# AdaLN block with causal attention: bias product in two halves, another order in the first and last unit, VectorE makes batch 1's unrounded rows from the banks, and another split of the last product

## What is computed

```python
mod = (silu(c) @ wmod).reshape(2, 6, 1, 256)          # sa, ca, ga, sb, cb, gb
ga, gb = ((2 * (g >= 0) - 1) * maximum(abs(g), 0.25) for g in (ga, gb))
h = layernorm(x) * (1 + ca) + sa
q, k = rotary((h @ Wq + bq) * 128 ** -0.5), rotary(h @ Wk + bk)
attn = softmax(causal(q @ k.T)) @ (h @ Wv + bv)        # 16 heads
x = x + ga * (attn @ Wo + bo)
h = layernorm(x) * (1 + cb) + sb
x = x + gb * qlinear(silu(qlinear(h, gate)) * qlinear(h, up), down)   # 704 hidden, integer weights less 128
```

## Time and profile before

| | |
|---|---|
| median of three runs | 1036.28 us |
| the profiled execution | 1035.97 us |
| its span | 1034.2 us |
| TensorE busy | 1006.3 us, 97% |
| VectorE, ScalarE, GpSimd busy | 771.6, 678.5, 620.3 us |
| granted clock of TensorE, mean | 0.997 |

### The profile page before, as it was taken

One profiled execution on the slowest core, in us unless ns is written; L12 is line 12 of the kernel. 1 busy time (PEld: TensorE's weight loads), 2 busy tenths in 40 slices (PEclk: granted clock), 3 DMA queues, 4 the chain that ended last, 5 costly groups with the idle time before them and its releaser, 6 DMA issues.

```text
span 1034.2 us, 20453 instructions
## 1 busy us (share of the span) xinstructions
PE 1006.3 (97%) x6318; PEld 903.9 (87%) x6318; DVE 771.6 (75%) x1664; ACT 678.5 (66%) x1447; POOL 620.3 (60%) x472
## 2 busy tenths in 40 slices
...
GB/s 253 120 41 70 44 32 42 72 44 38 37 35 71 51 41 32 67 44 41 41 43 60 41 41 42 71 51 31 32 70 51 41 37 91 62 62 42 1 42 43
DMA packets 41987, 56.03 MB, mean 54 GB/s; under 512 B 5508, under 2 KB 25028, under 8 KB 41924
## 3 DMA queue, kind: packets, MB, share of 16 engines
...
## 4 chain that ended last, share of the span: by engine, by line
PE 91%; DVE 2%; issue 2%; ACT 2%; POOL 1%; DMA 1%; SPq 0%; DVEq 0%; ACTq 0%; POOLq 0%
PE ps_r L1362 18%; PE ps_r L1361 18%; PE ps_r L1360 17%; PE ps_t L1519 12%; PE ps_s L1362 7%; PE ps_s L1361 7%; PE ps_s L1360 6%; PE ps_s L1367 2%; PE ps_s L1370 1%; PE ps_r L1369 1%; PE ps_r L1367 1%; PE ps_r L1458 1%; DMA wmod_a<-in_L_wmod 1%; POOL y L695 0%; ACT probs L907 0%
## 5 line engine op out<-in xcount | busy, mean ns | idle before, releaser
L651 POOL TENSOR_TENSOR swapped<-swapped,sin_sb 128x512 f32<-128x512 f32 x124 | 166.1, 1340 | 236.1 <-DMA swapped<-straight 235.6
L896 ACT ACTIVATE pT_hi<-ps_t 128x512 fp32r<-128x512 f32 (+3 forms) x384 | 186.8, 491 | 85.2 <-PE ps_t L1519 83.1
L1198 DVE TENSOR_TENSOR pT_lo<-ps_t,pT_hi 128x512 fp32r<-128x512 f32 (+3 forms) x384 | 202.3, 550 | 53.7 <-ACT pT_hi L896 53.6
L1263 DVE CUSTOM_DVE_ANT_0 ps_s<-ps_s,mask_wide 128x128 f32<-128x128 f32 (+7 forms) x256 | 194.5, 760 | 55.8 <-PE ps_s L1362 41.6
L661 POOL TENSOR_TENSOR qk_lo<-straight,qk_hi 128x512 fp32r<-128x512 f32 x124 | 162.2, 1322 | 112.3 <-ACT qk_hi L802 112.3
L907 ACT ACTIVATE probs<-ps_s,neg_max 128x128 f32<-128x128 f32 (+7 forms) x256 | 190.3, 743 | 44.1 <-DVE neg_max L1263 37.0
L1519 PE MATMUL ps_t<-ident,probs 128*128 128x128 f32 x1152 | 185.6, 274 | 6.5 <-DVE pT_lo L1198 5.9
L652 POOL TENSOR_TENSOR straight<-straight,cos_sb 128x512 f32<-128x512 f32 x124 | 180.9, 1459 | 0.0
L1126 DVE TENSOR_TENSOR straight<-straight,swapped 128x512 f32<-128x512 f32 x126 | 129.1, 1025 | 32.5 <-POOL straight L652 32.0
L1519 PEld LDWEIGHTS ps_t<-ident,probs 128*128 128x128 f32 x1152 | 134.3, 140 | 11.3 <-issue 4.9
L1360 PE MATMUL ps_s<-qk_hi 128*128 128x512 f32 (+3 forms) x384 | 139.9, 364 | 0.1
...
## 6 DMA issues: line engine op xcount, KB each, us to landing
...
```

The source lines that it names most:

```text
L651: pool.tensor_tensor(swapped[:, q, :], swapped[:, q, :], sin_sb[:, cs], ALU.mult)
L896: nc.scalar.activation(turned_at(ORDER[step], k0, k1)(pT_hi), ps_t[:, (T_FIRST[step] + j) % 2, 0:(k1 - k0) * P].rearrange("p (k q) -> p k ...
L1198: nc.vector.tensor_tensor(turned_at(t, k0, k1)(pT_lo), ps_t[:, (T_FIRST[step] + j) % 2, 0:(k1 - k0) * P].rearrange("p (k q) -> p k q", q=P ...
L1263: nc.vector.tensor_tensor_reduce(rows, rows, mask_wide[:, SEQ - n_keys:SEQ], -1.0, -MASKED, ALU.add, ALU.min, accum_out=neg_max[:, t:t + 1 ...
```

## The change

In unit 0 the bias product is made in two pieces, B0 ahead of the first turn and B1 behind the second; VectorE adds `bo` to the first and the first to the second; ScalarE's and VectorE's lists are reordered; the fourth exponential no longer waits for a turn. For batch 1, ScalarE writes only `hT_hi`; VectorE writes `h32` from the bank with one tensor_scalar (`h_plain`) ahead of each remainder, and TensorE waits for it (`plain_ready`) before it uses the bank again. In unit 31, W10 and W11 are made behind D1 and D2, W11 of unit 30 is summed in `ENDING`, and sums stand behind maxima and turns. In the feed-forward part the third chunk's turns stand one step later and its remainders ahead of steps 9 and 10. GpSimd converts the third part of the down weights earlier and leaves the last remainder to VectorE. The last down product goes by tiles 0 to 2 over the first four parts, then by tiles over the rest.

```diff
@@ -56,8 +56,8 @@
 EARLY_NORMAL_AT = {9: 3}
-TURN_AT = {7: (4,), 8: (5,), 13: (6,), 14: (7,)}
-LOW_AT = {0: (2,), 1: (3,), 8: (4, 5), 14: (6,), 15: (7,)}
+TURN_AT = {8: (4,), 9: (5,), 13: (6,), 14: (7,)}
+LOW_AT = {0: (2,), 1: (3,), 9: (4,), 10: (5,), 14: (6,), 15: (7,)}
@@ -96,13 +96,12 @@
     TENSOR_PLAN: """make:P0- make:P1- mods:1 scores:0 xn:4 make:K0+ xn:5 scores:1 make:Q0+ xn:6 xn:7 scores:2 scores:3
-        make:B turn:0.0 turn:1.0 scores:4 turn:1.1 make:K1+ turn:2.0 scores:5 make:Q1+ turn:3.0 turn:3.1 make:V0
+        make:B0 turn:0.0 turn:1.0 make:B1 scores:4 turn:1.1 make:K1+ turn:2.0 scores:5 make:Q1+ turn:3.0 turn:3.1 make:V0
         turn:4.0 scores:6 make:V1 turn:5.0 scores:7 turn:5.1""",
-    SCALAR_PLAN: """exp:0 out:K0+ xout:4 xout:5 exp:1 out:Q0+ xout:6 xout:7 exp:2 exp:3 high:K0+ high:Q0+ turn:0.0
-        turn:1.0 exp:4 turn:1.1 out:K1+ turn:2.0 exp:5 out:Q1+ turn:3.0
-        turn:3.1 turn:4.0 high:V0 high:K1+ high:V1 turn:5.0 exp:6 split:O turn:5.1 high:Q1+""",
-    VECTOR_PLAN: """max:0 max:1 xlow:4 xlow:5 max:2 max:3 add:K0+ xlow:6 xlow:7 add:Q0+ sum:B turn:0.0
-        turn:1.0 max:4 turn:1.1 gates:0 turn:2.0 max:5 turn:3.0 add:K1+ turn:3.1
+    SCALAR_PLAN: """exp:0 out:K0+ xout:4 xout:5 exp:1 out:Q0+ xout:6 xout:7 exp:2 turn:0.0 exp:3 turn:1.0 high:K0+ high:Q0+
+        turn:1.1 exp:4 out:K1+ turn:2.0 turn:3.0 exp:5 turn:3.1 out:Q1+ turn:4.0 high:V0 high:K1+ high:V1 turn:5.0 exp:6 split:O turn:5.1 high:Q1+""",
+    VECTOR_PLAN: """max:0 max:1 xlow:4 xlow:5 max:2 max:3 add:K0+ xlow:6 xlow:7 turn:0.0 sum:B0 turn:1.0 add:Q0+ sum:B1
+        turn:1.1 max:4 gates:0 turn:2.0 max:5 turn:3.0 add:K1+ turn:3.1
@@ -123,13 +122,13 @@
         make:P1- scores:3 turn:1.0 make:W00- make:X scores:4 turn:1.1 turn:2.0 make:W01- scores:5 make:D0 turn:3.0
-        make:W10- turn:3.1 turn:4.0 make:W11- scores:6 make:D1 turn:5.0 scores:7 make:D2 turn:5.1""",
+        make:D1 turn:3.1 scores:6 make:D2 turn:4.0 make:W10- scores:7 turn:5.0 make:W11- turn:5.1""",
     SCALAR_PLAN: """out:K0+ exp:7- turn:6.0- exp:0 out:Q0+ turn:7.0- turn:7.1- high:P0- turn:0.0 exp:1 exp:2
-        high:P1- turn:1.0 turn:1.1 exp:3 turn:2.0 exp:4 gated:0 out:D0 turn:3.0
-        exp:5 turn:3.1 turn:4.0 out:D1 exp:6 turn:5.0 out:D2 turn:5.1""",
+        high:P1- turn:1.0 turn:1.1 exp:3 turn:2.0 exp:4 gated:0 turn:3.0 out:D0
+        exp:5 turn:3.1 out:D1 turn:4.0 out:D2 exp:6 turn:5.0 turn:5.1""",
     VECTOR_PLAN: """largest:3 max:0 turn:6.0- turn:7.0- turn:7.1- max:1 low:P0- max:2 turn:0.0 moments:0
-        low:P1- max:3 sum:W00- turn:1.0 width:X max:4 turn:1.1 turn:2.0 sum:W01- max:5 turn:3.0 sum:W10- turn:3.1 turn:4.0
-        sum:W11- max:6 max:7 turn:5.0 turn:5.1"""}
+        low:P1- max:3 turn:1.0 sum:W00- width:X max:4 turn:1.1 turn:2.0 max:5 sum:W01- turn:3.0 turn:3.1
+        max:6 turn:4.0 max:7 turn:5.0 sum:W10- turn:5.1"""}
@@ -138,7 +137,7 @@
         silu:4 gu:3 silu:5 gu:4""",
-    VECTOR_PLAN: """turn:6.0- turn:7.0- turn:7.1- moments:1 newton:0 low:P0- low:P1- sum:W00- sum:W01-
+    VECTOR_PLAN: """turn:6.0- turn:7.0- turn:7.1- sum:W11-- moments:1 newton:0 low:P0- low:P1- sum:W00- sum:W01-
@@ -158,7 +157,7 @@
         what, name = token.rstrip("+-").split(":")
-        v = u + {"+": 1, "-": -1}.get(token[-1], 0)
+        v = u + token.count("+") - token.count("-")
@@ -679,7 +679,7 @@
-                        pool.wait_ge(attn_bias_ready, 1)
+                        pool.wait_ge(attn_bias_ready, 2)
@@ -742,9 +742,9 @@
             down_high(1)
+            down_high(2)
...
             gate_rows(2)
-            down_high(2)
@@ -760,6 +760,8 @@
                 low = gu_lo[:, n % GU, :]
+                if n == NCH * HM - 1:
+                    break
@@ -846,7 +848,8 @@
                 src, shift, gain = ps_t[:, n % 2, :], mod[:, k, b:b + 1], mod[:, KT + k, b:b + 1]
-                nc.scalar.activation(h32[:, n % 4, :], src, ACT.Identity, bias=shift, scale=gain)
+                if n < GROUPS4 // 2:
+                    nc.scalar.activation(h32[:, n % 4, :], src, ACT.Identity, bias=shift, scale=gain)
@@ -901,7 +904,7 @@
                 act.wait_ge(max_ready, ps.tiles(u, step + 1))
-                if u * NQ + step >= 3:
+                if u * NQ + step > 3:
@@ -1101,7 +1104,18 @@
             nc.vector.tensor_scalar(bq_s[:, :], cols[:, COL_BQ:COL_BQ + HEADS], SCALE, None, ALU.mult).then_inc(bq_ready, 1)
+            def h_plain(n):
+
+                k, b = n % KT, n // KT // 2
+                dve.wait_ge(hhi_ready, n + 1)
+                dve.wait_ge(hT_ready, n - 3)
+                nc.vector.tensor_scalar(h32[:, n % 4, :], ps_t[:, n % 2, :], mod[:, KT + k, b:b + 1], mod[:, k, b:b + 1],
+                                        ALU.mult, ALU.add).then_inc(plain_ready, 1)
+
             def h_low(n):
+                if n >= GROUPS4 // 2:
+                    h_plain(n)
+                    dve.wait_ge(plain_ready, n - GROUPS4 // 2 + 1)
@@ -1175,7 +1189,11 @@
                 dve.wait_ge(wo_all_ready, 32)
-                nc.vector.tensor_tensor(y[:, 0, :], ps_r[:, ps.bank(piece), 0:DIM], bo_wide[:, :], ALU.add)\
+                more = bo_wide[:, :]
+                if piece[1] == 1:
+                    dve.wait_ge(attn_bias_ready, 1)
+                    more = y[:, 0, :]
+                nc.vector.tensor_tensor(y[:, 0, :], ps_r[:, ps.bank(piece), 0:DIM], more, ALU.add)\
@@ -1194,6 +1212,9 @@
                 k0, k1 = groups_of(t)[j]
+                if u * T_UNIT + T_FIRST[step] + j == T_FIRST[1]:
+
+                    dve.wait_ge(hT_ready, GROUPS4)
@@ -1347,6 +1368,11 @@
                     finish(2 * j, 2, ps_r[:, j % 2, :].rearrange("p (t n) -> p t n", t=2))
+            last = NCH * HM - 1
+            dve.wait_ge(gu_hi_ready, last + 1)
+            dve.wait_ge(gu_split, last)
+            nc.vector.tensor_tensor(gu_hi[HLAST:P, last % GU, :], gu_at(last, HLAST),
+                                    gu_hi[0:HLAST, last % GU, :].bitcast(F32), ALU.subtract).then_inc(gu_split, 1)
@@ -1454,9 +1480,10 @@
                     pe.wait_ge(wo_all_ready, 32)
-                    for h in range(HEADS):
+                    half = HEADS // 2
+                    for h in range(piece[1] * half, piece[1] * half + half):
                         ins = nc.tensor.matmul(dst[:, 0:DIM], cols[:, COL_BV + h:COL_BV + h + 1].broadcast_to([P, P]),
-                                               wo_all[:, h, :], start=h == 0, stop=h == HEADS - 1)
+                                               wo_all[:, h, :], start=h % half == 0, stop=h % half == half - 1)
@@ -1514,6 +1541,7 @@
                     pe.wait_ge(hhi_ready, GROUPS4)
+                    pe.wait_ge(plain_ready, GROUPS4 // 2)
@@ -1556,6 +1584,8 @@
                     pe.wait_ge(hhi_ready, n - 1)
+                if n >= GROUPS4 // 2 + 2:
+                    pe.wait_ge(plain_ready, n - GROUPS4 // 2 - 1)
@@ -1698,12 +1728,13 @@
                 outs = [ps[:, j, 0:DIM] for ps in (ps_r, ps_t) for j in range(2)]
-                for m in range(HM):
-                    pe.wait_ge(gu_split, (NCH - 1) * HM + m + 1)
-                    for t in range(4):
+                for t, parts in ((0, range(0, 4)), (1, range(0, 4)), (2, range(0, 4)), (0, range(4, HM)),
+                                 (1, range(4, HM)), (2, range(4, HM)), (3, range(0, HM))):
+                    for m in parts:
+                        pe.wait_ge(gu_split, (NCH - 1) * HM + m + 1)
                         ins = down_part(outs[t], t, NCH - 1, m, wide_weights)
-                        if m == HM - 1:
-                            ins.then_inc(down_made, 1)
+                    if HM - 1 in parts:
+                        ins.then_inc(down_made, 1)
```

More of the change, by code:

```diff
@@ L408, in build @@
         hT_ready = sem("hT_ready")
+        plain_ready = sem("plain_ready")
         shift_ready = sem("shift_ready")
```

2 lines of the change are left out of this document (1 added, 1 removed).

## The result

The changed kernel takes 1041.87 us in the median of six runs (1039.49 to 1044.47); the kernel before took 1036.24 us in six runs beside them (1035.83 to 1037.36). The ratio is 1.0056, 95% interval 1.0042 to 1.0071: **slower by 5.6 us**, where the forecast's sum said 3.1. The spread grew as well, from 1.5 to 5.0 us. The profiled execution is the slowest of the six, 1044.47 us with a span of 1042.6 us.

The account below looks back on a forecast made before the run. The prediction took TensorE, busy 1006.3 of 1034.2 us, as the bound; its terms 0.5 + 1.8 + 2.1 - 1.3 gave +3.1 us, forecast as 1039.2 us, range 1036.0 to 1041.6 us.

Parts of the forecast that it names:

- term C: Third feed-forward chunk: GpSimd's remainders queue behind a late release and TensorE stands still 3.3 us before step 12; +2.1 us.
- term A: First unit: VectorE's new row operations delay turns, the split bias product removes a wait, Q1's chain decides the end; +0.5 us.
- Term B: Last unit and ending: later sums and a tensor_scalar held by GpSimd's product delay the statistics and feed-forward start; +1.8 us.
- Term D: Last down product: VectorE makes the last remainder and tiles finish earlier, so the first finishing operation starts sooner; -1.3 us.
- third rival: Third chunk: the granted clock falls behind the new standstill and later steps lose about 1.7 us; 1041.1 us, chance 20%.
- first and second rivals: First: the waits go and stay gone, 1033.6 us, 11%; second: GpSimd's queue holds nobody in the third chunk, 1036.5 us, 14%.

Follow-up runs that it names:

- a_alone_again: A second profiled execution of the kernel before with all of the first unit's change and nothing else: 1035.87 us, with a short low-clock stretch (3.4 us).
- after_look_3: A third profiled execution of the whole changed kernel: 1040.87 us, with a low-clock stretch of 3.4 us near 35 us.
- after_again: A second profiled execution of the whole changed kernel: 1040.75 us, with a low-clock stretch of 3.4 us near 35 us.
- a_alone: The kernel before with all of the first unit's change and nothing else: median 1039.05 us, ratio 1.0026.
- b_alone: The kernel before with the new lists of unit 31 and the ending, and GpSimd's earlier conversion of down weights: median 1037.99 us, ratio 1.0016.
- d_alone: The kernel before with the new last down product alone: median 1035.57 us, ratio 0.9995.

## Why the prediction was off

The direction was right, by the mechanisms named; the size was not, and 1041.87 us lies just outside the range. Two steps failed. The sum priced term C's standstill at its length alone and put the clock behind it at nothing, as a rival of 20%; the runs show 1.6 us for it. And term A was the schedule of one execution with a short low-clock stretch, where a long one costs 1.8 to 2.9 us more. Step by step:

- **Term A (+0.5).** In executions with a short low stretch it is close: +0.55, +0.69 and +1.09 us at unit 1's turn (a_alone_again, after_look_3, after_again), with the wait ahead of it as described. The step failed where it took the schedule of one profiled execution for all. The whole part is +2.7 us in the median of a_alone: the long stretch near 35 us, which costs the kernel before 0.3 us at most, costs this one 1.8 to 2.9 us. How often it is long was not measured. The row that priced VectorE's new operation, 0.68 us, was also low: it measured 0.80 to 0.81 us. The figure of the Trainium skill that I had weighed against it (VectorE: DVE Perf Modes, the section on the TRN2 errata), 0.66 us, was further off.
- **Term B (+1.8).** Right, place by place: D1 waited 1.08 us for a forecast 1.2, the small tensor_scalar was held to 0.74 us, and the part from unit 31's turn to the feed-forward start grew by 1.8 us in all three profiles. It had no term for the clock behind its own wait either, and in b_alone that came to 0.95 us.
- **Term C (+2.1).** Right: 3.09 us of wait for a forecast 3.3, and +2.0 us.
- **Term D (-1.3).** VectorE's first finishing operation came 1.1 us earlier relative to step 18. d_alone gave only 0.5 us: in its trace the outputs' transfers end 0.3 us later behind the last operation than before, and the rest lies within its interval.
- **The third rival (20%).** This is the step that failed in the sum. It was priced rightly, 1.7 us for a measured 1.6, and its chance was too low: four of five profiled standstills had it. With it the sum is 4.8 us, for 5.6 us measured. I held that no row showed an idle stretch in the middle that did this, and let that count against it; there was no row of a standstill of 3 us without a fall either. The Trainium skill (TensorE: Matmul & The Clock Gate, the section on HAM oscillation) warned of it, and the traces agree in four of five.
- **The first and second rivals.** Out. TensorE waited for GpSimd, and the gains in the first unit were spent before unit 1.

What remains open: why the clock falls among the narrow matmuls in one execution and behind them in the next was not tried, nor whether moving those matmuls would end the long stretches. Nor is it shown how the 5.6 us of the median divide: the three profiles of the changed kernel lie at 4.8, 4.9 and 8.5 us above the first profile before.

## What to carry to other kernels

Waiting on an engine that is not the bottleneck is a reserve. The kernel before had 2.2 us of it on VectorE between two maxima, and a late start vanished in it; work moved there cost 0.6 to 1.1 us at unit 1 in executions with a short low-clock stretch and 2.9 to 3.4 us in those with a long one. Place helper work of an in-order engine in the stretch where it waits for somebody else, never behind the release; here the same two subtractions were worth +2 us on one side of it and nothing on the other. And when an edit makes a standstill of the matmul engine of this length, count the clock behind it with it, and profile more than one execution: the first profile alone would have put 2.9 us on the first unit that another shows as 0.7 us.

## What the chip showed beyond that

- A standstill of 3.1 us of TensorE was followed by a granted clock of 0.50 for 3.4 us (once 6.8 us) in four of five profiles, at a cost of 1.6 us (2.8 us); with twelve matmuls in it whose output nobody reads, 0.23 us apart, the clock stayed at 1.00 in the one profile taken.
- Shorter waits were sometimes followed by a fall too: one of 2.25 to 2.27 us for normalised rows in one of the four profiles that have it (low for 6.8 us, at a cost of 0.95 us), and the pair of 1.05 and 0.78 us at unit 31's end in 3 of the 13 profiles that have it (low for 3.4 us; the feed-forward part began 0.2 us later).
- A VectorE tensor_scalar from a 128x512 PSUM bank with two per-partition operands took 0.80 to 0.81 us, against 0.68 to 0.69 us for a tensor_tensor that reads a bank of that size.
- A VectorE addition of two SBUF tensors, 128x512, took 0.69 us alone and 1.72 to 1.76 us when GpSimd was at work; a tensor_scalar of four columns 0.17 and 0.74 us.
